# Attention on TensorE: the maxima product moved ahead of the two score products in every unit

## The reference, cut to what matters

```python
q = einsum('bnd,hde->bhne', query, Wq) * scale      # 16 heads of 64
k = einsum('bmd,hde->bhme', query, Wk)
v = einsum('bmd,hde->bhme', query, Wv)
logits = einsum('bhne,bhme->bhnm', q, k)            # 1024 x 1024 for each batch and head
attn = softmax(logits, axis=-1)
out = einsum('bhnm,bhme->bnhe', attn, v)
return dot(swapaxes(out, -1, -2).reshape(B, N, E * H), Wp) + bp
```

## Time and profile before

| | |
|---|---|
| median of 3 executions | 1117.27 us (1116.45 to 1118.58) |
| the profiled execution | 1117.38 us, span of its instructions 1115.6 us |
| TensorE, matmul | busy 1038.6 us (93%), 7983 instructions |
| TensorE, weight loads | busy 855.6 us (77%) |
| VectorE / GpSimd / ScalarE | 839.0 us (75%) / 683.8 us (61%) / 652.1 us (58%) |
| mean granted TensorE clock | 0.971 of full |

### The profile page before, as it was taken

The page is one execution under the profiler, slowest core; times in us unless marked ns, Lnnn a source line. Parts: engine busy times, 40 slices in busy tenths (PEclk is TensorE's granted clock), DMA queues, the critical chain, the costliest instruction groups (busy, mean ns, idle before and its releaser), DMA issues. The chain is left out here.

```text
span 1115.6 us, 25325 instructions
## 1 busy us (share of the span) xinstructions
PE 1038.6 (93%) x7983; PEld 855.6 (77%) x7983; DVE 839.0 (75%) x1699; ACT 652.1 (58%) x1319; POOL 683.8 (61%) x663
## 2 busy tenths in 40 slices
PE   6799999999999999999999999687997599999996
PEld 4678888888888888888888888455685477777774
DVE  5877887877787787787787787355765569888896
ACT  4556565565555555656565565454444587766774
POOL 4166876876876876777777786401221277767772
PEclk9999999999999999999999999988898799999998
DMA  5243533533633533534534433110000011212111
GB/s 125 51 97 75 123 85 71 130 78 71 130 79 74 129 78 80 120 78 88 112 78 97 107 75 67 32 42 1 0 1 1 20 60 63 88 56 75 57 38 38
DMA packets 57041, 80.09 MB, mean 72 GB/s; under 512 B 25956, under 2 KB 38048, under 8 KB 55968
## 3 DMA queue, kind: packets, MB, share of 16 engines
q1 hardware_dynamic: 54780, 78.97, 30.0%
q10 hardware_dynamic: 2220, 0.59, 0.3%
HBM read 19.43 MB, written 1.11 MB: 18 GB/s over the span
## 5 line engine op out<-in xcount | busy, mean ns | idle before, releaser
L617 POOL TENSOR_TENSOR probs_lo<-probs 128x512 f16<-128x512 f32 x384 | 420.1, 1108 | 195.2 <-ACT probs L450 193.5
L481 DVE TENSOR_REDUCE maxes<-bank_m 128x1 f32<-128x512 f32 x512 | 353.0, 690 | 138.2 <-PE bank_m L288 134.4
L450 ACT ACTIVATE probs<-bank_s 128x512 f32<-128x512 f32 x512 | 296.9, 608 | 266.1 <-PE bank_s L376 265.3
L369 PE MATMUL bank_s<-qa,ka 128*128 128x512 f32 x512 | 226.0, 441 | 5.7 <-DVE v_parts L528 2.5
L288 PE MATMUL bank_m<-ka,qa 128*128 128x512 f32 x512 | 204.9, 400 | 3.6 <-DMA ka<-tk_lo 3.3
L376 PE MATMUL bank_s<-qb,kb 65*128 65x512 f32 x512 | 205.8, 402 | 2.2 <-DMA qb<-negmax 2.2
L311 PE MATMUL bank_o<-v_now,probs 128*128 128x129 f16 x2048 | 200.6, 220 | 1.0 <-ACT o_parts L416 1.0
L1368 POOL TENSOR_TENSOR hidden_lo<-rectified,hidden_hi 128x512 fp32r<-128x512 f32 x112 | 155.6, 1406 | 60.7 <-ACT hidden_hi L1513 49.9
L311 PEld LDWEIGHTS bank_o<-v_now,probs 128*128 128x128 bf16 x2048 | 175.4, 97 | 21.9 <-issue 20.6
L307 PE MATMUL bank_o<-v_now,probs_lo 128*128 128x65 f16 x2048 | 184.7, 193 | 0.0
L288 PEld LDWEIGHTS bank_m<-ka,qa 128*128 128x128 f32 x512 | 158.6, 310 | 28.6 <-DMA ka<-tk_lo 3.7
(11 more groups left out here) (250 smaller groups left out, 1681.6 us busy)
## 6 DMA issues: line engine op xcount, KB each, us to landing
qa<-tq_hi SPq DMA_DIRECT2D x64, 256.0 KB, 3.8
v_now<-v_parts SPq DMA_DIRECT2D x32, 260.0 KB, 2.3
ka<-tk_hi SPq DMA_DIRECT2D x32, 256.0 KB, 2.9
ka<-tk_lo SPq DMA_DIRECT2D x32, 256.0 KB, 4.9
kb<-tk_hi SPq DMA_DIRECT2D x32, 256.0 KB, 5.0
qb<-tq_lo SPq DMA_DIRECT2D x32, 256.0 KB, 5.2
gates_on_all<-gate_rows SPq DMA_DIRECT2D x8, 1024.0 KB, 4.7
e_raw<-in_L_ffn_ew_dram SPq DMA_DIRECT2D x16, 256.0 KB, 3.0
```

Of the source, the lines that this page charges most:

```text
L369: nc.tensor.matmul(bank_s[u % 2][:], ka[h][:, ks], qa[h][:, qs], start=True, stop=False)
L450: nc.scalar.activation(probs[:, c, u, :], bank_s[u % 2][:], ACT.Exp, scale=SCALE).then_inc(exp_done, 1)
L481: nc.vector.tensor_reduce(maxes[:, j // 2, j % 2:j % 2 + 1], bank_m[j % 2][:], AX.X, ALU.max).then_inc(m_reduced, 1)
L617: nc.gpsimd.tensor_tensor(probs_lo[:, c, u, :], p, hi, ALU.subtract).then_inc(lo_pool, 1)
```

## The change

In the step of TensorE's program the maxima product, with its wait for `head_in` and the one for `m_reduced` inside `max_scores`, moves from behind the two score products to the start of the unit, ahead of the wait for `exp_done`. Everything else keeps its order: the products with V, the projections, the turn and the product with `Wp` still end the unit. The other engines' programs are the same.

```diff
@@ -363,6 +363,10 @@
                 h, c = s // 2, s % 2
                 for u in range(UNITS):
                     n = 32 * i + 8 * s + u
+                    if m := max_at(i, s, u, first, last):
+                        if m[2] == 0:
+                            pe.wait_ge(head_in[1 - h], HEAD_DMAS * (i + 1 + h))
+                        max_scores(m[0], m[2], MAX_N * m[1] + m[2])
                     if not (first and s == 0 and u < 2):
                         pe.wait_ge(exp_done, n - 1)
                     ks, qs = slice(u * P, (u + 1) * P), slice(c * CH, (c + 1) * CH)
@@ -374,10 +378,6 @@
                         if c == 0:
                             pe.wait_ge(tail_in[h], TAIL_DMAS * (i + 1))
                     nc.tensor.matmul(bank_s[u % 2][:], kb[h][0:E + 1, ks], qb[h][0:E + 1, qs], start=False, stop=True).then_inc(s_filled, 1)
-                    if m := max_at(i, s, u, first, last):
-                        if m[2] == 0:
-                            pe.wait_ge(head_in[1 - h], HEAD_DMAS * (i + 1 + h))
-                        max_scores(m[0], m[2], MAX_N * m[1] + m[2])
                     if not (first and s == 0):
                         pi, psn = (i, s - 1) if s else (i - 1, 3)
                         times_v(pi, psn, PV_TO[u - 1] if u else 0, PV_TO[u])
```

## The result

| | before | after |
|---|---|---|
| median | 1116.86 us (4 executions) | 1133.17 us (1132.05 to 1134.51, 4 executions) |
| ratio to before | | 1.0141, 95% interval 1.0124 to 1.0158 |
| the profiled execution | 1117.38 us, span 1115.6 | 1132.05 us, span 1130.2 |
| predicted | | 1135.7 us (1129 to 1142) |

Slower by 16.3 us; the forecast was 18.3. The two profiled executions lie 14.7 us apart.

The account below looks back on a forecast made before the run. TensorE's pace was taken to bound the first attention, some 650 us of the span. Terms 18.4 + 0.6 + 0.5 + 0.2 - 1.4 = +18.3 us on 1117.4 gave 1135.7 us, range 1129 to 1142.

Parts of the forecast that it names:

- Term 1: Maxima product opening a unit behind short V, turn or Wp products: weight load uncovered, 153 x 0.12 = +18.4 us.
- same-time rival: Maxima product's load is taken ahead under V products or costs only the first score product's: 1117.3 us; chance 0.08.
- Term 2: Exp wait before units 3 and 7: seven products in the chain either way, so the 0.29 us stays; change 0.
- faster rival: Exp wait before units 3 and 7 gets the maxima product's stream as cover, 24 us go: 1112 us; chance 0.04.
- Term 3: Maxima product's waits now hold the score products too: reductions 0, next head's load in unit 5 +0.6, late heads +0.5, +0.2.
- Term 4: Row of maxima reaching unit 0's second score product by DMA: 0.7 us more room, two waits shrink, -1.4 us.
- the two late heads: Maxima product of unit 5 held by late head loads, at 55.98 and 77.00: +0.5 and +0.2 us.
- The slower rival: Wp product waits for ScalarE's copy, room 0.3 falling to 0.06 us; overdrawn in 30 places, +6: 1142 us; chance 0.14.

Follow-up runs that it names:

- near_ahead: Changed kernel, with 128 neighbouring columns of qa as the maxima product's weights instead of every fourth (output not the reference's): 1117.64 us, ratio 1.0001.
- near_behind: Kernel before the change, with neighbouring columns of qa as the maxima product's weights instead of every fourth (output not the reference's): 1114.85 us, ratio 0.9968.
- copies_behind: Kernel before the change, with ScalarE's two copies of o after the exp of units 1 and 5 instead of 0 and 4: 1096.65 us, ratio 0.9831.
- copies_ahead: Changed kernel, with ScalarE's two copies of o after the exp of units 1 and 5 instead of 0 and 4: 1123.29 us, ratio 1.0051.

## Why the prediction was right

**Term 1, the load out of cover: right in kind, a little large.** The rows gave 0.12 us for an opening; measured are 0.44 against 0.32 in the step shown, and 0.434 against 0.319 as medians from 100 to 660 us. In the stretches 0.08 to 0.11 us of it are left, some 1.05 of the 1.17 us a pair: 153 x 0.105 is 16 us instead of 18.4. Taking the length of the load away takes 15.5 us away, of which some 13 are the order's (near_ahead and near_behind together). The same-time rival fails by its own sign, M to SA 0.44 and not 0.32. The estimate that made it possible was one M, at 55.98, that had happened to wait for something else.

At the end, behind the turn of pair 15, seven openings are 0.84 us and 0.88 were measured, but that agreement is luck. Pair 15 itself takes 1.45 us more (from its first turn to that of its own output, 39.70 against 38.25), and the rest of the program, which the edit doesn't touch, half a us less. In pair 15 two things were not in the sum: the Wp products, below, and the last exp wait of step 2, which grows by 0.24 us: units 5 to 7 have no M there, and M of unit 4 has moved out of the chain from SB of unit 4 to SA of unit 7, so that the count of products is four instead of five.

**Term 2, the exp waits stay: right.** Seven products lie between SB 0 and SA 3 in both, and 0.44, 0.93, 1.43 us on ScalarE's side are unchanged. The faster rival is out. That the chain runs over the copies is shown by copies_behind, where it goes with them.

**Term 3, waits that M carries: right kind, a little small.** The reduction's wait is there and hides in the exp wait (0.31 against 0.29 to 0.30). The next head's wait came as said:

```profile
329.83 0.61 PE L288 MATMUL bank_m<-ka,qa 128*128 128x512 f32 x1
...
330.50 0.40 PE L380 MATMUL bank_s<-qb,kb 65*128 65x512 f32 x1
330.93 0.62 PE L288 MATMUL bank_m<-ka,qa 128*128 128x512 f32 x1
331.39 0.40 PE L373 MATMUL bank_s<-qa,ka 128*128 128x512 f32 x1
```

```profile
325.86 1.23 SPq L198 DMA_DIRECT2D ka<-tk_lo  x1
```

The fourth DMA issued at 325.86 lands some 5 us later, M of unit 5 goes at 330.93, and behind it the exp wait of unit 7 is gone. From the start of the V products to the next ones (328.45 to 333.30) this stretch takes 4.85 us, against 4.60 before (323.60 to 328.20): 0.25 (0.23 as the median of the pairs), of which 0.11 is the opening. So some 0.12 us is left of the wait, where I had 0.04, because M's load lies open behind the wait as well (0.46 to SA), which I hadn't counted. That is 1.7 us instead of 0.6 in 14 pairs. M of unit 5 in step 0, the other head's, doesn't wait: its stretch grows by its two openings alone.

**Term 4, the row of maxima: right in sign, too small.** The forecast took 0.7 us off each of the two waits; both are gone whole. The pair with the wait at 340.05 (42.32 us long) has no counterpart, 1.05 us. The stretch with the wait at 82.14, from the V products at 78.86 to the next ones, took 6.30 us, and in the changed kernel (from 78.66) 4.72: 1.58 us less, or 1.7 without its opening. The row's DMA, before and after:

```profile
78.44 0.51 SPq L206 DMA_DIRECT2D qb<-negmax  x1
```

```profile
77.75 0.51 SPq L206 DMA_DIRECT2D qb<-negmax  x1
```

Before, SB went 3.70 us after that issue, as the row came. Now it goes at 80.71, 2.96 us after it, and doesn't wait: the row took less time on its way than before, which the edit doesn't order. So what goes beyond the forecast here is luck, 1.0 us; with the other pair term 4 is -2.7 us instead of -1.4.

**The start: the sign was wrong.** Up to the first turn in pair 1 I had some +0.7 us (the two late heads 0.7, six openings 0.7, less 0.7 of the wait at 82.14); it was -1.63. One part is the 1.58 us of that wait. The other is that the changed kernel comes to its first step earlier. The row of maxima for it, made by a stretch of the program that the edit doesn't touch, is sent 1.3 us sooner, before and after:

```profile
43.61 0.52 SPq L206 DMA_DIRECT2D qb<-negmax  x1
```

```profile
42.31 0.52 SPq L206 DMA_DIRECT2D qb<-negmax  x1
```

M of unit 5 in the first step follows by as much, at 54.69 and not at or after 55.98:

```profile
54.69 0.62 PE L288 MATMUL bank_m<-ka,qa 128*128 128x512 f32 x1 [2.12 <-DMA ka<-tk_lo]
```

The stretches at the low clock are other ones, too. Before they lay from 20 to 23 us, ahead of the first step, and from 58 to 60; after from 49 to 51, where TensorE had a DMA to wait for in any case, and from 56 to 58 us. That the early 1.3 us are the clock's is my reading. How much moves between executions of one kernel is seen in the four of the changed one: spans of 1130.2, 1130.2, 1132.5 and 1132.7 us, with mean granted clocks of 0.971 and 0.968. That spread is as large as what the forecast missed at the start (2.3 us), and larger than what it missed by in all (2.0 us). The nearness of 18.3 and 16.3 us is in part luck: term 1, term 4 and the early start came out below the forecast, term 3 and pair 15 above it.

**The slower rival** came in pair 15 alone. In pair 6 ScalarE's copy of the turned output ends at 309.40 and the Wp product loads at 309.51: the 0.06 us of room that I gave it were 0.1. Pair 15 has no projections ahead of its Wp products, and there the copy was late already. Before and after:

```profile
677.35 0.38 PE L331 MATMUL bank_x<-wp_pair,o_turned 128*128 128x128 f32 x1
```

```profile
691.42 0.38 PE L331 MATMUL bank_x<-wp_pair,o_turned 128*128 128x128 f32 x1 [0.25 <-ACT o_turned L420]
```

It follows the last product by 0.42 us before and 0.65 after, and so twice: +0.46 us of the 6 that the rival had.

## What to carry to other kernels

A weight load costs next to nothing as long as a long stream runs over it (here 310 ns under 512 columns), so ask of each reordering which load it puts behind a short product, and read that load's price at a place where it happens to be uncovered already. Count the products between the two ends of a waiting chain before and after: if the count is the same, the wait is; look at the last rounds apart, where products are missing. And a wait can be a cover for others: the same edit to ScalarE's order was worth 20 us in one order of TensorE and 10 us in the other, because behind the wait that went others of the same size stood ready.

## What the runs showed of the hardware

A load of 128 x 128 fp32 weights took 190 ns with neighbouring columns, 196 with every second, 310 with every fourth (16 bytes apart) and 318 with every eighth; uncovered, the difference between 190 and 310 ns is 0.12 us on the distance of the matmuls, and under a 512-column stream some 4 ns.

VectorE's residue of `probs` (line 558, 128x512) took 0.68 us at best, and with GpSimd at its own residues (line 617) beside it 1.43 us in the row shown; its mean was 802 ns before the change, 912 after and in copies_behind, and 997 in copies_ahead. GpSimd's stayed at 1.10 us in all of them. I had taken VectorE's time as fixed. That the two engines hinder one another is what the rows suggest; no run here took one of them away.
